# A graph attention layer and a quantised feed-forward layer: edge scatters issued between the weight chunks

## The reference, cut to what matters

```python
mask = jnp.full((N, N), -jnp.inf, dtype=dtype)
mask = mask.at[src, dst].set(w[edge_type - 1])      # 6528 edges, the last of equal ones stands
diag = jnp.diagonal(mask)
mask = mask.at[idx, idx].set(jnp.where(jnp.isneginf(diag), w[3], diag))
scores = jnp.einsum('hnd,hmd->hnm', q2, k2) * scale + mask[None]
```

## Time and profile before

| | us |
|---|---|
| median of 3 runs (339.83 to 342.97) | 340.94 |
| the profiled execution | 342.69 |
| its span | 340.7 |
| TensorE busy | 326.9 |
| VectorE busy | 237.8 |
| GpSimd busy | 191.5 |
| ScalarE busy | 180.0 |

### The profile page before, as it was taken

The page is one execution under the profiler, slowest core; times in us unless marked ns, Lnnn a source line. Parts: engine busy times, 40 slices in busy tenths (PEclk is TensorE's granted clock), DMA queues, the critical chain, the costliest instruction groups (busy, mean ns, idle before and its releaser), DMA issues.

```text
span 340.7 us, 5921 instructions
## 1 busy us (share of the span) xinstructions
PE 326.9 (96%) x2045; PEld 297.1 (87%) x2045; DVE 237.8 (70%) x610; ACT 180.0 (53%) x338; POOL 191.5 (56%) x253
## 2 busy tenths in 40 slices
PE   5999999999999999979999999999999999999985
PEld 5899998788999999969999999999999878887544
DVE  4857989763075554269985978879797874697674
ACT  3734257464743333323356968678586774253333
POOL 6786666557787677776966393563726857000000
PEclk9999999999999999999999999999999999999999
DMA  7996345576144334652331231403213210000005
GB/s 253 379 406 248 118 145 167 188 237 190 49 123 139 131 108 148 247 179 62 123 118 58 76 123 62 125 11 115 74 52 123 64 63 0 2 0 0 2 0 185
DMA packets 16762, 41.70 MB, mean 122 GB/s; under 512 B 3440, under 2 KB 7392, under 8 KB 16736
## 3 DMA queue, kind: packets, MB, share of 16 engines
q1 hardware_dynamic: 13824, 38.87, 33.3%
q0 software_dynamic: 2064, 1.80, 1.7%
q10 hardware_dynamic: 848, 0.70, 0.6%
HBM read 37.99 MB, written 3.37 MB: 121 GB/s over the span
## 4 chain that ended last, share of the span: by engine, by line
PE 57%; POOL 13%; issue 12%; DMA 9%; DVE 7%; ACT 2%; POOLq 0%; DVEq 0%; ACTq 0%
PE PS L699 33%; POOL codes L406 9%; DMA codes<-ecol,place 7%; PE PS L856 5%; PE PS L844 4%; PE PS L832 4%; PE PS L680 2%; DMA scratch<-codes 2%; PE PS L991 2%; DVE scratch L1201 2%; POOL ring L389 1%; PE PS L1016 1%; PE PS L690 1%; DVE scratch L1200 1%; PE PS L768 1%
## 5 line engine op out<-in xcount | busy, mean ns | idle before, releaser
L389 POOL TENSOR_TENSOR ring<-stage,ring 128x256 fp32r<-128x256 f32 x128 | 97.9, 799 | 40.5 <-ACT ring L471 38.3
L699 PE MATMUL PS<-XT,ring 128*128 128x384 f32 x528 | 94.1, 336 | 2.8 <-DVE AT L1100 2.3
L699 PEld LDWEIGHTS PS<-XT,ring 128*128 128x128 f32 x528 | 91.3, 188 | 3.8 <-DVE AT L1100 2.9
L406 POOL DMA_INDIRECT codes<-ecol,place x51 | 59.2, 1161 | 27.0 <-issue 17.2
L471 ACT ACTIVATE ring<-stage 128x1024 fp32r<-128x1024 f32 x52 | 54.3, 1056 | 1.6 <-DMA stage<-in_weights 1.5
L571 ACT ACTIVATE scratch<-scratch,smx 128x384 f32<-128x384 f32 x48 | 29.0, 605 | 19.1 <-DVE smx L1223 19.1
L1138 DVE TENSOR_TENSOR ring<-stage,ring 128x1024 fp32r<-128x1024 f32 x20 | 24.5, 1224 | 18.2 <-issue 13.1
L699 PE MATMUL PS<-QT,ring 128*128 128x384 f32 x192 | 35.6, 339 | 0.0
L699 PE MATMUL PS<-AT,ring 128*128 128x384 f32 x192 | 35.2, 338 | 0.0
L699 PE MATMUL PS<-ring,AT 128*128 128x512 f32 x144 | 34.6, 394 | 0.0
L699 PEld LDWEIGHTS PS<-AT,ring 128*128 128x128 f32 x192 | 33.0, 188 | 1.5 <-issue 1.5
(11 more groups left out here) (207 smaller groups left out, 484.9 us busy)
## 6 DMA issues: line engine op xcount, KB each, us to landing
stage<-in_weights SPq DMA_DIRECT2D x56, 512.0 KB
V<-in_w_gate_up SPq DMA_DIRECT2D x4, 512.0 KB, 6.9
codes<-scratch SPq DMA_DIRECT2D x3, 576.0 KB, 13.4
scratch<-codes POOLq DMA_DIRECT2D x3, 576.0 KB, 6.5
X<-in_x SPq DMA_DIRECT2D x3, 512.0 KB, 5.0
out<-X SPq DMA_DIRECT2D x4, 384.0 KB, 2.6
scratch<-in_w_gate_up SPq DMA_DIRECT2D x2, 512.0 KB
V<-in_w_down SPq DMA_DIRECT2D x5, 176.0 KB, 5.9
```

What stands on the lines that cost most here:

```text
L389: ins = pool.tensor_tensor(ring[1][:, slot, piece], stage[:, slot % STAGE, piece], ring[0][:, slot, piece].bitcast(F32), ALU.subtract)
L406: pool.indirect_dma_start(codes[b].rearrange("(n a) -> n a", a=1), bass.IndirectOffsetOnAxis(ap=place[:, t:t + 1], axis=0), ecol[:, VAL, t ...
L699: ins = pe.matmul(outs, lhs[a], rhs[b], start=start and n == 0, stop=stop and n == 2, skip_group_check=True)
```

## The change

Four edits, all on the edges' way to the tables. The blocks are laid out in the order of the scatter, so that scatter t takes column t. The values of a list are then every third column (three strided instructions instead of three over 17 columns). The positions are computed in seven parts (`placed`), part q over the columns 8q to 8q + 7 once the groups 2q and 2q + 1 are counted; parts 0 to 4 stand in the steps 1 to 5 of VectorE's first loop behind `tile_low`, parts 5 and 6 in step 6. On GpSimd scatter c - 3 stands behind `low(c)` for c from 3 to 9, and the other 44 follow. Each scatter waits for its part of the positions. What each list gets, and in which order, is the same as before.

```diff
@@ GpSimd, values
             for b in range(LISTS):
-                part_b = slice(b * PER_LIST, (b + 1) * PER_LIST)
-                ins = pool.tensor_scalar(ecol[:, VAL, part_b], ecol[:, TYP, part_b], 16.0 ** (b + 1), 0.0,
-                                         ALU.mult, ALU.add)
+                val_b, typ_b = (ecol[:, r, 0:LISTS * PER_LIST].rearrange("p (i b) -> p i b", b=LISTS)[:, :, b]
+                                for r in (VAL, TYP))
+                ins = pool.tensor_scalar(val_b, typ_b, 16.0 ** (b + 1), 0.0, ALU.mult, ALU.add)
@@ GpSimd, scatters
             pool.wait_ge(y_ready, NT + 1)
+            def scatter(t):
+
+                i, b = t // LISTS, t % LISTS
+                pool.wait_ge(place_ready, min(t // 8 + 1, 7))
+                if i:
+                    pool.wait_ge(scattered[b], 16 * i)
+                else:
+                    pool.wait_ge(codes_blank[b], 16)
+                pool.indirect_dma_start(codes[b].rearrange("(n a) -> n a", a=1),
+                                        bass.IndirectOffsetOnAxis(ap=place[:, t:t + 1], axis=0),
+                                        ecol[:, VAL, t:t + 1], None, bounds_check=N * N - 1, oob_is_err=False
+                                        ).then_inc(scattered[b], 16)
+
             for c in range(CIV + 2):
                 low(c, c % RING)
-
-
-            pool.wait_ge(place_ready, 1)
-            for i in range(PER_LIST):
-                for b in range(LISTS):
-                    t = b * PER_LIST + i
...
+                if c >= 3:
+                    scatter(c - 3)
+            for t in range(CIV - 1, LISTS * PER_LIST):
+                scatter(t)
@@ VectorE, positions
+            def placed(q):
+
+                dve.wait_ge(key_used, min(2 * q + 2, GROUPS))
+                used = slice(8 * q, min(8 * q + 8, LISTS * PER_LIST))
+                dve.scalar_tensor_tensor(place[:, used], dup[:, used], 2.0 ** 20, ecol[:, KEY, used], ALU.mult, ALU.add
+                                         ).then_inc(place_ready, 1)
+
             for s in range(8):
                 tile_low(s, s, V_BANK[s], AT, BIAS_V + s)
+                if 1 <= s <= 6:
+                    placed(s - 1)
                 for g in (2 * s, 2 * s + 1):
                     if g < GROUPS:
                         once(g)
                 if s == 6:
-                    dve.wait_ge(key_used, GROUPS)
-                    used = slice(0, LISTS * PER_LIST)
-                    dve.scalar_tensor_tensor(place[:, used], dup[:, used], 2.0 ** 20, ecol[:, KEY, used], ALU.mult, ALU.add
-                                             ).then_inc(place_ready, 1)
+                    placed(6)
@@ layout of the inputs
-    edge = [np.concatenate([np.asarray(a, np.int32), np.full(EC * P - E, f, np.int32)]).reshape(EC, P)
+    order = [b * PER_LIST + i for i in range(PER_LIST) for b in range(LISTS)] + list(range(LISTS * PER_LIST, EC))
+    edge = [np.concatenate([np.asarray(a, np.int32), np.full(EC * P - E, f, np.int32)]).reshape(EC, P)[order]
```

## The result

The changed kernel takes 344.38 us in the median of 20 runs (lowest 342.68), the kernel before 341.83 in 20 runs on the same chips. The ratio is 1.005, 95% interval [1.0028, 1.0072]: slower by 0.5%, where 339.0 and at most 341.4 were forecast. Six of the 20 runs, 348 to 366 us, were disturbed; the ratios and the counts of runs by their level leave such runs out, the medians do not. The profiled execution took 344.37 us, its span is 342.6, 1.9 above that of before.

What follows compares the result with a forecast made beforehand. TensorE, busy 326.9 of 340.7 us, was taken as the bound, its later stands fed by VectorE's codes wait. Terms: -2.6 returned, +0.7 VectorE cost, -1.9 in sum; against the 340.94 median, 339.0 us, range 337.0 to 341.4.

Steps and rivals of the forecast that it cites:

- The stand at chunk 30: TensorE's 2.34 us stand at 150.12, traced to VectorE's wait for the codes; claimed to vanish with an earlier read-back.
- the ends of 2.3 to 2.9: Range on the 2.6 us forecast to come back on TensorE at chunk 30 and the scores.
- the 0.28 us ahead of the scores: TensorE's stand before the first scores at 170.78, traced to the same codes wait and counted in the 2.6 us gain.
- the prediction's 145.3: Time in us by which codes could arrive with nearly the same effect; 6 of the 9.25 us were called unneeded.
- rival (b): Scatters overfill GpSimd's slots ahead of chunk 9, TensorE waits on a subtraction between 30 and 60 us; 346.6 us, chance 0.07.
- 1.66: Forecast us of GpSimd per early scatter: 1.16 on average plus 0.19 and 0.30 beside it.
- about nothing: Forecast loss for chunk 4, whose 3.85 us lead follows `low(4)`; scatter 0 was said to fit the 2.57 us gap.
- 5.2 us of lead less 1.1 hide it: Chunk 5 is ready at 32.80, wanted by TensorE at 38.00; `low(5)` 1.1 us late was said to cost 0.
- VectorE's term: Position parts delay VectorE between steps 2 and 4; new TensorE stand of 0.7 us, ends 0.1 and 1.3.
- the 0.93 of the sum: Forecast VectorE us for `placed(1)` at 0.17 plus `placed(2)` at 0.76, before subtracting the 0.25 margin.
- Rival (a): VectorE pieces plus one feed-forward scaling collision with a shifted subtraction (0.8 us) cost 2.1 against 2.6; 340.4 us, chance 0.17.
- The lead at `keys(9)`, 0.25 us: Margin between VectorE's last read of `once(7)` at 37.54 and TensorE's `keys(9)` near 37.79, subtracted from VectorE's cost.

Runs made afterwards that it cites:

- the filler: Changed kernel plus 13 unused matmuls of 384 columns on TensorE ahead of `keys(8)`, inside the stand; ratio to the kernel before 1.0038, median 342.95 us.
- two with the wait: GpSimd's subtraction of chunk 6 waits for the first feed-forward scaling step: changed kernel with seven parts, 0.9934; with positions in two parts, 0.9966, to the kernel before.
- the best version: Changed kernel with positions in two parts and six early scatters, none behind `low(4)`; ratio to the kernel before 0.994, run again 0.9925, median 339.90 us.
- the first one with the wait: Changed kernel, seven parts, GpSimd's subtraction of chunk 6 waiting for the first scaling step; ratio to the kernel before 0.9934, median 340.16 us.
- the version with two parts: Changed kernel with positions in two parts (columns 0 to 7 in step 1, other 43 in step 6), early scatters kept; ratio to the kernel before 1.0071.

## Why the prediction was wrong

**What bounds the kernel: right.** The stand at chunk 30 hung on the codes and went away; 2.8 us came back where 2.6 were summed, within the ends of 2.3 to 2.9. A part of that closeness is luck: the 0.28 us ahead of the scores, which the sum counts, did not come back, and the stand of 2.34 was worth 2.8. That only the first part of the scatters' lead counts was right too: three early scatters give as much as five, and with one, whose codes let VectorE go on at 145.23, TensorE had no stand at chunk 30, as the prediction's 145.3 has it.

**GpSimd: the right number by two errors.** `low(5)` came 31.06 - 29.98 = 1.1 us later, as worked out, and TensorE did not wait for any subtraction, which was the sign of rival (b). But an early scatter took 1.2 us of GpSimd (from 33.89, the end of `low(5)`, to 35.07) and not 1.66, and scatter 0 did not fit its gap: it waited for its position, started at 25.76 and made `low(4)` 0.38 us late, where "about nothing" was said. The read-back was issued at 133.26 and not at 129.5, since GpSimd followed TensorE's 4.7 us; it was early enough.

**The failed step is that the moved subtractions were costed at 0.** The prediction said of `low(5)`: "5.2 us of lead less 1.1 hide it; cost on the path 0", and gave the later ones no cost on VectorE at all. I asked only who waits for their results. Nobody does. But they moved in time against VectorE. Its long scaling came at 34.82 instead of 34.44, and `low(6)` came at 35.07, directly behind scatter 2, instead of 34.70 behind an idle GpSimd; the scaling then took 2.9 us more. VectorE began the step 0.13 us sooner than before; `placed(1)`, which met the late `low(4)`, cost it 0.4 and the two-column scaling, beside the late `low(5)`, another 0.1. The late `low(5)` can do it alone: without `placed(1)` it made VectorE 0.5 us late, and the loss stayed. Whether `placed(1)` could do so too, with `low(5)` on time, was not tried. With `low(5)` back in its place, or no scatter ahead of `low(6)`, or `low(6)` held back for the scaling, the loss is gone.

**VectorE's term was mis-sized: 0.7 us where it was 4.7.** `placed(1)` measured 0.49 us where 0.17 was taken, `placed(2)` 0.15 where 0.76 was, together less than the 0.93 of the sum. What I left out is the instruction between them. Rival (a) named this very collision and priced it at 0.8 us, one piece of GpSimd's; it took 3.26 - 0.40 = 2.9, the whole subtraction. Before, the scaling and `low(6)` started at 34.44 and 34.70, a near miss of a quarter of a microsecond that stood in VectorE's and GpSimd's timelines. The chance of 0.17 for (a) went to a version that was still faster than before; none of the rivals had the result.

**A stand of TensorE was costed at its length.** The clock dip behind it added 1.57 us in the profiled execution, nine of 14 runs have the lower mean clock that goes with it, and the filler shows that it belongs to the stand. The lead at `keys(9)`, 0.25 us, was the right place to look, and a place with so little lead makes every VectorE delay of step 2 and 3 a full loss.

**The spread of the runs was read in part.** The kernel before ran 93 times beside the experiments. Of these runs 17, at 343.8 to 345.0, have a mean clock of 0.994 or 0.995, and the other 76, at 339.6 to 343.6, have 0.997 or more. So the spread is not only that of the landings: in some runs the clock falls as well. Six experiments have a profile with no stand over 0.7 us near 38 us and none at chunk 30 (two with the wait, two of the best version, the one without a scatter behind `low(5)`, the one with three early); in their 63 runs no mean clock is under 0.997. That the clock falls behind a long stand at chunk 30 fits this, and the gain would then be more than the stand in such runs; it is not shown, since no such run was profiled. The best version stays within 0.5 us in all its 21 runs and the first one with the wait within 0.13; in the three others single runs still lie 1.4 to 4 us above the median, with a mean clock of 0.999 or 1.

**What stays open.** The same scaling takes 0.88 us when it is asked for inside a piece (two kernels). It takes 0.40 when it is asked for 0.18 to 0.27 us ahead of the pieces with GpSimd idle before them (five kernels), and 3.26 to 3.30 when it is asked for 0.24 to 0.29 us ahead and a scatter or a memset runs until they start (four kernels). Beside a scatter whose pieces are held back it takes 0.40 (two kernels). What fits every trace is that neither the lead nor the scatter alone matters but pieces directly behind another instruction of GpSimd's; the mechanism inside is not shown, nor how long a gap would let the scaling in.

The Trainium skill, SBUF — State Buffer, section "SBUF: two separate sides", has VectorE's 2-port instructions and GpSimd's exclude each other for a whole instruction. The scaling reads one SBUF tensor and its factors, so the rule bears on it only if it runs as what that section calls a 2-port instruction, which no run here tells. The 0.88 us agree with the rule, one piece waited for. The 3.26 us go beyond it: it is four instructions in a row. The measurement decides.

## What to carry to other kernels

When an instruction of GpSimd moves, ask not only who waits for it but also which VectorE scaling, or instruction with two SBUF inputs, it now runs beside; near misses in the two timelines are part of the profile. Price such a meeting at GpSimd's whole run of instructions, not at one, and price a stand of TensorE with the slow clock behind it. Moving work into gaps pays until the wait that it feeds is gone; here three moved scatters bought all of it, and with two parts, leaving out the slot that was too short turned 0.7% slower into 0.6 to 0.75% faster.

## What the runs showed of the hardware

- A VectorE scaling of 128x352 float32 (0.40 us) took 3.26 to 3.30 us beside four GpSimd subtractions of 0.7 us each that followed a scatter at once (in one kernel with a memset between), in four kernels; where the subtractions were held back it took 0.40 beside the scatter; a scaling of 128x2 took up to 0.67 instead of 0.17 beside one.
- A position part of 8 columns with two SBUF inputs took 0.15 to 0.22 us at most places and 0.41 to 0.77 at others, all of these beside a GpSimd subtraction; three columns took 0.64 beside one. Beside a subtraction it can also take 0.18 (the kernel with parts only, at 35.33).
- After 2.9 us of TensorE standing with 0.4 us of work in between, the granted clock was 0.71 over the next 5.9 us in the profiled execution of the changed kernel, and 1.00 in that of the version with two parts, which stood 2.8 us with as much work in between. Nine of 14 runs of the changed kernel and nine of 11 of the other have a mean clock of 0.995 or less.
